# A graph network on one core: two destination tiles per addition, count stores on the ScalarE queue, first loads of pass one moved

## What is computed

```python
h = relu(layernorm(x))                        # layer 0: gated, weighted sum
g = sigmoid(h @ W0_gate + b_gate) * (h @ W0)
x = x + segment_sum(edge_weight[:, None] * g[dst], src)
h = relu(layernorm(x))                        # layer 1
x = x + segment_sum(h[src], dst) @ W1.T + b1
# layer 2: messages of both ends, summed by dst, and an update product
# layer 3: hypergraph layer: sum by dst, scale, sum back by src, batch norm, ReLU
```

## Time and profile before

| | |
|---|---|
| median of 3 runs | 2562.01 us (2561.71 to 2567.41) |
| the profiled execution | 2568.25 us, its span 2566.4 us |
| PE busy in the span | 2309.7 us, 90% |
| DVE busy | 1596.8 us, 62% |
| ACT busy | 1181.9 us, 46% |
| counting pass | tile 0 complete at 140 us, tile 48 at 1282 us |
| pass one's first matmul | 1344.86 us |
| mean granted PE clock | 0.962 of 2.4 GHz |

### The profile page before, as it was taken

One profiled execution on the slowest core, in us unless ns is written; L12 is line 12 of the kernel. 1 busy time (PEld: TensorE's weight loads), 2 busy tenths in 40 slices (PEclk: granted clock), 3 DMA queues, 4 the chain that ended last, 5 costly groups with the idle time before them and its releaser, 6 DMA issues.

```text
span 2566.4 us, 70830 instructions
## 1 busy us (share of the span) xinstructions
PE 2309.7 (90%) x27901; PEld 1990.4 (78%) x27901; DVE 1596.8 (62%) x3655; ACT 1181.9 (46%) x2490; POOL 46.3 (2%) x52
## 2 busy tenths in 40 slices
PE   3489999999899998999939999899998999999997
PEld 2368878887787887877838888788887888887886
DVE  8689999999999998999962333234333112122223
ACT  3488778877777876888831222122221000011112
POOL 3300000000000000000000000000000000000000
PEclk9599999999999998999979999999998999999998
DMA  7589999999999999999989999999997999999998
GB/s 197 119 166 220 208 209 210 219 210 207 209 186 221 207 203 193 204 218 214 217 197 228 290 289 290 262 260 259 257 258 204 290 289 290 273 245 244 261 266 193
DMA packets 1608984, 589.35 MB, mean 230 GB/s; under 512 B 964422, under 2 KB 1605450, under 8 KB 1608567
## 3 DMA queue, kind: packets, MB, share of 16 engines
q1 hardware_dynamic: 1604869, 579.88, 101.8%
q0 software_dynamic: 1600, 4.92, 0.7%
...
## 4 chain that ended last, share of the span: by engine, by line
PE 49%; SPq 22%; DMA 11%; DVE 6%; issue 5%; ACT 5%; POOL 1%; DVEq 0%; ACTq 0%; POOLq 0%
PE ps L676 33%; SPq L419 13%; SPq L446 8%; DMA counts_by_source<-stage 7%; PE ps L589 2%; ACT stage L1208 2%; PE ps L591 2%; PE ps L590 2%; ACT stage L1193 2%; DVE X L924 2%; PE ps L614 2%; DMA a_turned<-counts_by_source 2%; PE ps L615 2%; PE ps L616 2%; PE ps L597 1%
## 5 line engine op out<-in xcount | busy, mean ns | idle before, releaser
L1208 ACT CAST stage<-ps 128x784 f16<-128x784 f32 x784 | 655.7, 836 | 105.5 <-DMA counts_by_source<-stage 73.3
L676 PE MATMUL ps<-Ha,a_tiles 128*128 128x258 f16 x4606 | 523.8, 273 | 6.9 <-DVE Ha L994 6.9
L614 PE MATMUL ps<-hot_c,hot_r 128*128 128x98 f16 x3136 | 508.2, 211 | 14.1 <-DVE hot_c L912 7.5
L676 PEld LDWEIGHTS ps<-Ha,a_tiles 128*128 128x128 f16 x4606 | 449.9, 98 | 73.4 <-DVE Ha L994 7.6
L615 PE MATMUL ps<-hot_c,hot_r 128*128 128x98 f16 x3136 | 502.1, 210 | 0.0
L616 PE MATMUL ps<-hot_c,hot_r 128*128 128x98 f16 x3136 | 500.4, 210 | 0.0
L589 PE MATMUL ps<-g_in,wt 128*128 128x128 f16 x2401 | 431.5, 222 | 38.1 <-DVE X L924 21.7
L1193 ACT CAST stage<-ps 128x392 f16<-128x392 f32 x784 | 398.3, 508 | 141.9 <-PE ps L597 141.9
L590 PE MATMUL ps<-g_in,wt 128*128 128x128 f16 x2401 | 429.7, 222 | 0.0
L591 PE MATMUL ps<-g_in,wt 128*128 128x128 f16 x2401 | 429.6, 222 | 0.0
L924 DVE SCALAR_TENSOR_TENSOR X<-ps,X 128x512 f32<-128x512 f32 (+1 forms) x637 | 392.1, 649 | 45.5 <-PE ps L591 45.3
...
## 6 DMA issues: line engine op xcount, KB each, us to landing
a_tiles<-counts_by_source SPq DMA_DIRECT2D x147, 1600.0 KB, 13.7
counts_by_source<-stage SPq DMA_DIRECT2D x49, 1600.0 KB, 8.1
...
wt<-stage SPq DMA_TRANSPOSE x98, 10.9
...
```

The source lines that it names most:

```text
L614: mm(into(0), rows_, codes(0), start=v == 0, stop=True, skip_group_check=True)
L676: last = mm(ps[:, sum_bank(ph, j, c), 0:PARTS], a_slot(ph, c, i), moving[:, i], start=i == 0, stop=i == TILES - 1)
L1208: a.copy(stage[:, b, 0:2, 0:TILES, u * SET_COLS:(u + 1) * SET_COLS], of).then_inc(s("hi_done"), 1)
```

## The change

1. **Two destination tiles per addition.** `sum_four` now sums a pair of tiles into the same PSUM bank (24 matmuls in place of 12), and DVE adds once. PE has one four behind a hot (`fours_at`): six in odd tiles, seven in even ones. The additions of a pair start one tile after it is complete. `wt` becomes six half-tile places (`HOMES`), `g_in` four, and each transpose is split into two (24 and 25 blocks).
2. **Counts stored from ACT.** `store_counts` issues the store of tile j-1 on ACT's queue behind unit 0 of tile j. ACT waits for `stored` and the high parts' transposes at unit 0, for the low parts' at unit 2.
3. **Keys by group.** To make room, `meta` and `meta_w` go to DRAM (`edge_groups`) while they are made, and SP reloads 128 KB once per pair of tiles, two groups ahead.
4. **Pass one's first loads.** Tiles 1 and 2 are loaded once tiles up to 47 are stored and turned, tile 0 once tile 48 is, and 3 to 5 once all is added. `first_tiles` waits for each load where it first uses it, in the order 1, 2, 0, 3.

The diff, cut to its core:

```diff
+PARTED = FULL + WEIGHTS * TILES
+FIRST = 6
+HALF_TILES = (range(0, 4 * FIRST), range(4 * FIRST, TILES))
+HOMES = (((0, 1), (2, 3)), ((4, 5), (0, 2)), ((1, 3), (4, 0)), ((5, 2), (1, 4)), ((3, 0), (5, 1)), ((2, 4), (3, 5)))
+KEYS = 2 * P
+GROUP_WORDS = KEYS + WEIGHTS * P
...
-def summed_at(h):
-
-    return range(2 * h, min(2 * h + 2, FOURS))
+def fours_at(c, h):
+
+    if c % 2:
+        return range(h - 1, h) if 1 <= h <= FIRST else range(0)
+    return range(FIRST + h, FIRST + h + 1) if FIRST + h < FOURS else range(0)
+
+
+def pair_of(k, c):
+
+    return k * (SLOTS // 2) + c // 2
+
+
+def home(c, half):
+
+    return HOMES[c // 2 % len(HOMES)][c % 2][half]
...
+        groups = nc.dram_tensor("edge_groups", (GROUPS + 1, P, GROUP_WORDS), F16).ap()
...
-        meta, o = at("meta", [P, GROUPS, 2, P // 2, 2], F16, base0)
-        meta_w, o = at("meta_w", [P, WINDOWS // 2, WEIGHTS, 2], F16, o)
+        meta, o = at("meta", [P, 2, GROUP_WORDS], F16, base0)
...
-        stage, o = at("stage", [P, 2, 1 + WEIGHTS, FULL, P], F16, o)
+        stage, o = at("stage", [P, 2, PARTED, P], F16, o)
         wt_at = o
-        wt, o = at("wt", [P, 2, WEIGHTS, TILES, P], F16, o)
-        g_in, o = at("g_in", [P, 2, 2 * P], F16, o)
+        wt, o = at("wt", [P, 6, WEIGHTS, len(HALF_TILES[1]), P], F16, o)
+        g_in, o = at("g_in", [P, 4, 2 * P], F16, o)
...
+            def store_groups(m):
+
+                lot = batch(m)
+                sp.wait_ge(s("meta_w"), m + 1)
+                sp.wait_ge(s("keys_in"), 16 * (m + 1))
+                to = groups[lot.start:lot.stop].rearrange("n e x -> e n x")
+                sp.dma_start(to[:, :, 0:KEYS], keys_b[:, m % 2]).then_inc(s("meta_stored"), 16)
+                sp.dma_start(to[:, :, KEYS:], weights_b[:, m % 2]).then_inc(s("meta_stored"), 16)
...
+                if m >= 2:
+                    sp.wait_ge(s("meta_stored"), 32 * (m - 1))
+                sp.dma_start_transpose(keys_b[:, m % 2].rearrange("e n (a x) -> e (n a) x", a=2),
                                        pre[:].rearrange("q n a e -> q (n a e)")).then_inc(s("keys_in"), 16)
                 if m:
-                    sp.wait_ge(s("meta_w"), m)
+                    store_groups(m - 1)
...
+            sp.wait_ge(s("meta_stored"), 32)
+            for n in range(2):
+                sp.dma_start(meta[:, n], groups[n]).then_inc(s(f"meta_in{n}"), 16)
...
-                    b = c % 2
-                    if later(j, 2):
-                        sp.wait_ge(s("four_done"), (j - 1) * FOURS)
-                    for a, done in enumerate(("hi_done", "lo_done")):
+                    b, pair = c % 2, pair_of(k, c)
+                    if b:
+                        sp.wait_ge(s("hot_ready"), j * TILE_HOTS + TILE_HOTS)
+                        to = (c // 2 + 2) % 2
+                        of = groups[pair + 2] if isinstance(j, int) else groups[bass.ds(pair + 2, 1)].rearrange("a e x -> (a e) x")
+                        sp.dma_start(meta[:, to], of).then_inc(s(f"meta_in{to}"), 16)
+
+                    if b and later(j, 2):
+                        sp.wait_ge(s("four_done"), (pair - 1) * FOURS + FIRST)
+                    elif later(j, 4):
+                        sp.wait_ge(s("four_done"), (pair - 1) * FOURS)
+
+                    def turn(a, done, turned):
+
                         part = slice(a * P, (a + 1) * P)
                         sp.wait_ge(s(done), (j + 1) * HALVES)
-                        sp.dma_start(g_in[:, b, part], slab(g_dram, j)[:, part]).then_inc(s(f"g_loaded{b}"), 16)
-                        sp.dma_start_transpose(wt[:, b, a], stage[:, b, 1 + a, 0:TILES].rearrange("p i d -> p (i d)")).then_inc(s(f"wt_in{b}"), 16)
-                    sp.dma_start(two_tiles(j), stage[:, b, 0].rearrange("p (i a) d -> p i (a d)", a=2)).then_inc(s(f"stored{b}"), 16)
+                        sp.dma_start(g_in[:, c % 4, part], slab(g_dram, j)[:, part]).then_inc(s(f"g_loaded{b}"), 16)
+                        for half, tiles in enumerate(HALF_TILES):
+                            first = FULL + a * TILES + tiles.start
+                            sp.dma_start_transpose(wt[:, home(c, half), a, 0:len(tiles)],
+                                                   stage[:, b, first:first + len(tiles)].rearrange("p i d -> p (i d)")).then_inc(s(turned), 16)
+
+                    turn(0, "hi_done", f"hi_turned{b}")
+                    turn(1, "lo_done", f"lo_turned{b}")
 
                 tiles_loop(sp, hand_on, 0)
+
+                def load_counts(ph, j, c):
+
+                    q = load_at(ph, c) % SLOTS
+                    sp.dma_start(a_tiles[:, q].rearrange("p (i a) d -> p i (a d)", a=2), two_tiles(j)).then_inc(s(f"a_in{q}"), 16)
+
+                sp.wait_ge(s("stored1"), 16 * (TILES // 2))
+                sp.wait_ge(s("stored0"), 16 * (TILES // 2))
+                sp.wait_ge(s("lo_turned1"), 32 * (TILES // 2))
+                sp.wait_ge(s("hi_turned1"), 32 * (TILES // 2))
+                for j in (1, 2):
+                    load_counts(1, j, j)
...
                 counts_stored(sp)
-                sp.wait_ge(s("added"), FOURS * TILES)
+                sp.wait_ge(s("lo_turned0"), 32 * GROUPS)
+                sp.wait_ge(s("hi_turned0"), 32 * GROUPS)
+                load_counts(1, 0, 0)
+                sp.wait_ge(s("added"), FOURS * GROUPS)
+                for j in (3, 4, 5):
...
-                def sum_four(t, b, g):
-
-                    n, e = t * FOURS + g, (b + g) % 2
-                    if not (isinstance(t, int) and t * FOURS + g < 2):
-                        pe.wait_ge(s("added"), n - 1)
+                def sum_four(n, cp, g, both=True):
+
+                    f, e = n * FOURS + g, (cp + g) % 2
+                    if not (isinstance(n, int) and n * FOURS + g < 2):
+                        pe.wait_ge(s("added"), f - 1)
+                    half = int(g >= FIRST)
                     for i in range(4 * g, min(4 * g + 4, TILES)):
                         o = ps[:, 6 + e, (i % 4) * P:(i % 4 + 1) * P]
-                        mm(o, wt[:, b, 0, i], g_in[:, b, 0:P], start=i % 4 == 0, stop=False, skip_group_check=True)
-                        mm(o, wt[:, b, 0, i], g_in[:, b, P:2 * P], start=False, stop=False, skip_group_check=True)
-                        last = mm(o, wt[:, b, 1, i], g_in[:, b, 0:P], start=False, stop=True, skip_group_check=True)
+                        for b in range(1 + both):
+                            c = 2 * cp + b
+                            at_ = wt[:, home(c, half), :, i - HALF_TILES[half].start]
+                            mm(o, at_[:, 0], g_in[:, c % 4, 0:P], start=i % 4 == 0 and b == 0, stop=False, skip_group_check=True)
+                            mm(o, at_[:, 0], g_in[:, c % 4, P:2 * P], start=False, stop=False, skip_group_check=True)
+                            last = mm(o, at_[:, 1], g_in[:, c % 4, 0:P], start=False, stop=True, skip_group_check=True)
                     last.then_inc(s("four_done"), 1)
...
+                def loaded(n, b):
+
+                    pe.wait_ge(s(f"hi_turned{b}"), (n + 1) * 32)
+                    pe.wait_ge(s(f"lo_turned{b}"), (n + 1) * 32)
+                    pe.wait_ge(s(f"g_loaded{b}"), (n + 1) * 32)
...
-                        if later(j, 2):
-                            sums(j - 2, c % 2, k * (SLOTS // 2) + c // 2, h)
+                        for g in fours_at(c, h):
+                            if not isinstance(n, int) or n >= 0:
+                                if g == 0:
+                                    loaded(n, 0)
+                                    loaded(n, 1)
+                                sum_four(n, cp, g)
...
-                        for j in range(TOGETHER):
-                            pe.wait_ge(s(f"a_in{load_at(1, j) % SLOTS}"), (load_at(1, j) // SLOTS + 1) * 16)
                         for part in range(SET):
                             pe.wait_ge(s("h_ready1"), part + 1)
-                            for j in range(TOGETHER):
+                            for j in (1, 2, 0, 3):
+                                if part == 0:
+                                    pe.wait_ge(s(f"a_in{load_at(1, j) % SLOTS}"), (load_at(1, j) // SLOTS + 1) * 16)
                                 for i in range(part * SET, (part + 1) * SET):
                                     last = mm(ps[:, sum_bank(1, j, j), 0:PARTS], a_slot(1, j, i), Ha[:, i], start=i == 0, stop=i == TILES - 1, skip_group_check=True)
-                                if part == SET - 1:
-                                    last.then_inc(s("sum_done1"), 1)
+                                if part == SET - 1 and j == 3:
+                                    last.then_inc(s("sum_done1"), TOGETHER)
...
+                    if c % 2 == 0 and h == 0:
+                        slot = c // 2 % 2
+                        dve.wait_ge(s(f"meta_in{slot}"), k * 24 + (c // 4 + 1) * 16)
...
```

(19 more changed lines are left out.)

93 lines of the change are left out of this document (50 added, 43 removed).

## The result

| | before | with the change |
|---|---|---|
| median | 2562.15 us (4 runs) | 2610.56 us (4 runs, 2604.13 to 2611.99) |
| ratio | 1 | **1.018**, 95% interval 1.0161 to 1.0198 |
| span of the profiled execution | 2566.4 us | 2610.2 us |
| first to last instruction, by stage: up to tile 0 complete | 140.0 | 145.7 (+5.7) |
| tiles 1 and 2 | 46.5 | 47.9 (+1.4) |

The account below looks back on a forecast made before the run. DVE was taken to bound the counting pass at about 23.07 us a tile, PE close behind. Terms -53.8 - 10.7 + 3.5 - 16.8 = -77.8 us gave 2484 us against the median of 2562.01; range 2458 to 2545.

Parts of the forecast that it names:

- Transposes beside the store: SP's transposes, counting pass: store delays them by half its length, SP busy 19.5 us per tile, 1.2 spare, no cost.
- The check by rate: DMA traffic per tile, counting pass: 4.9 MB at 292 GB/s take 17 us, so tiles of 21.9 us hold them.
- Additions, -53.8: Tiles 3 to 48: 13 DVE additions per pair instead of 26, tiles 21.9 us instead of 23.07, -53.8 us.
- Store on ACT: ACT's queue behind unit 0: the store's issue, 0.45 us, counts in full, raising a tile from 21.25 to 21.7 us.
- Rival B: ACT's store issue at unit 1 held 2.5 us behind a half transpose: tiles 24.4 us, 2602 us in all; chance 0.18.
- Rival A: Counting pass: DMA engines become the bound, transposes and store hardly overlapping; tiles 22.8 us, 2526 us in all; chance 0.21.
- Tile 2, -10.7: Counting pass start: tile 2 also has no sums and falls from 28.8 to 18.1 us, -10.7 us.
- Start, +3.5: Before the first hot: stores of keys and weights on SP's queue delay weight transposes, +3.5 us, ends 2.7 and 7.
- Pass one, -16.8: Pass one's start: earlier loads let PE begin at 1328.1 instead of 1344.86, -16.8 us.
- Rival C: Pass one does not start earlier, load 3 colliding with 4 and 5 or the split late: 2501 us; chance 0.05.
- End of the pass: From the last tile's completion to pass one's first load, 37.1 us: all of it stays, change nothing.

Follow-up runs that it names:

- b_act_store: Kernel before, with only the counts' store moved from SP's to ACT's queue, behind unit 0 of the next tile: ratio 1.0031.
- b_split: Kernel before, with only each transpose of 49 blocks split into 24 and 25: ratio 1.0125, mean tile 24.35 us.
- b_light_adds: Kernel before, with each DVE addition over half of its columns: one execution, 2569.0 against 2554.8 us, mean tile 24.00 us.
- a_sp_store: Changed kernel, with the counts' store put back last on SP's queue, behind the transposes: ratio 1.0100, mean tile 24.64 us.
- b_first_loads: Kernel before, with only the change's earlier first loads of pass one: ratio 0.9935, mean tile 23.74 us.
- b_loads_again: Kernel before, with only pass one's earlier first loads, measured a second time: ratio 0.9928, mean tile 23.76 us.

## Why the prediction was wrong

Measured: 2610.56 us, outside the range of 2458 to 2545.

**The step that failed** is in "Transposes beside the store": "If the store (1600 KB, 5.6 us at 292) delays the transposes by half its length, SP is busy 19.5 us per tile", and with it "It fits with 1.2 us to spare. Cost taken: none." The store delayed the transposes by its whole length and a little more. In b_act_store, where only the store was moved, SP's part of a tile grew from 16.5 to 22.7 us. In the tile of the change shown above it is 23.8, of which the halving is 1.4 (17.9 in b_split against 16.5) and the store 5.9. The landing took 5.7 in place of 3.4. The place was free 29.5 us behind the tile's end, where 22.9 had been worked out, and ACT asked for it after 23.7 (24.1 worked out): 1.2 us to spare became 5.75 us of stop.

The check by rate, "A tile's 4.9 MB at 292 are 17 us, so 21.9 us hold them", missed the same thing. 292 was the rate of a store alone; no kernel with the whole store moved more than 216 GB/s over 200 us, with transposes among the bytes. The row that gave the nearer bound stood beside it: 217 for transposes alone.

- **Additions, -53.8.** Right as far as the engines go: 21.5 us with a small store. Wrong as a gain, since b_light_adds shows that relief for DVE alone brings nothing. Nor was 23.07 the mean of before: it is 23.82, with some long tiles among the regular ones, which I took as fixed. The 46 tiles gained nothing and lost 50.7. The means even flatter the change: tiles 25 and 37, 29.95 and 32.99 us before, are 25.43 and 26.31 with it, and the other 44 went from 23.47 to 24.88.
- **What makes it slower, not just no faster.** By the tiles' means: halving +0.53 (b_split), then additions and keys with the store still last on SP +0.29 (a_sp_store), then the store's place on ACT +0.28. These are single profiles, taken in one order of adding the parts, and differ by about 0.1 for one kernel; b_act_store (1.0031) shows that the last part is nearly free while DVE paces. "The halving adds two instructions to it" was one sentence without a price, and it is the largest of them. Why a split costs stays open.
- **Store on ACT.** The issue took 0.39 us, near the 0.45 forecast; all 49 took 0.38 to 0.44, and 24 of them lie wholly inside SP's transposes, as that at 465.59 lies inside the 8.18 us from 459.44. **Rival B**, ACT held in it, is refuted. The trace disagrees with what the prediction drew from the Trainium skill's exclusive lock (Perfetto Trace Analysis, "DMA Instruction - HWDGE (DVE, Sync)").
- **Rival A** was the right mechanism, by the Trainium skill's rule that queues share the same 16 engines (DMA: Bandwidth & Descriptors, "Issuing engines are not separate DMA queues"), which the trace bears out: a transpose of 7.5 us, or 8.2 in halves, became 14.55 beside the store. I worked out 22.1 for it "if not a byte overlaps" and 24.6 with a landing of 8.1 us, and took 22.8; measured 24.92. The upper end was nearer, and there rival A too ends slower, a side that I kept almost wholly for rival B (0.18 of 0.20).
- **Tile 2, -10.7.** Tile 2 was 18.3 us as forecast, but tile 1 became 29.6: SP was in tile 0's transposes, two of 14 us that met the stores issued at 145.75 and 163.55, until 174.6. One long tile moved one place ahead; +1.4 in all.
- **Start, +3.5.** Measured 5.7, inside its ends of 2.7 and 7, but one pair of profiles does not settle it: b_first_loads and b_loads_again, the same kernel, complete tile 0 at 153.47 and 138.76. Why is open; the ratios compare runs that were measured side by side.
- **Pass one, -16.8.** PE starts at 1390.04, 0.06 us behind the split's end, in place of 17.1 behind it: that step is right, and b_first_loads confirms it alone. **Rival C**'s collision of loads is refuted. But the split came 4.5 us later behind the last tile, so 12.6 were gained. That is the term "End of the pass", put at nothing: the last tile's high parts took 12.38 us to transpose beside the store that ACT issued at 1337.69, in place of 7.92, and its last transpose was issued 22.8 us behind the tile in place of 17.0. (By its own rows the 13 fours of the pair before take up to 13 x 1.41 = 18.3 us, not "under 18"; they took 1.34 each.)
